# Maxima and scores of an attention step in another order on TensorE

## What is computed

```python
scores = jnp.einsum('bhqd,bhkd->bhqk', q, k) / np.sqrt(HD).astype(np.float32)
scores = jnp.where(attn_mask[:, None, None, :], scores, -jnp.inf)
attn = jax.nn.softmax(scores, axis=-1)
out = jnp.einsum('bhqk,bhkd->bhqd', attn, v)
out = out.transpose(0, 2, 1, 3).reshape(x.shape[0], x.shape[1], H)
x = residual + out @ wo + bo
...
ff = jax.nn.gelu(h @ ff_w1 + ff_b1, approximate=False) @ ff_w2 + ff_b2
return residual + ff
```

```python
scores = jnp.einsum('bqgrh,bkgh->bgrqk', q, k) * (1.0 / np.sqrt(HD))
a = jax.nn.softmax(scores, axis=-1)
out = jnp.einsum('bgrqk,bkgh->bqgrh', a, v).reshape(b, n, d)
...
x = x + g1 * _gqa_attn(h, wq, wk, wv, wo)
```

## Time and profile before

| | us |
|---|---|
| median of 3 runs | 4138.36 |
| lowest and highest | 4135.44 and 4140.47 |
| profiled execution, its own time | 4144.66 |
| its span from first to last instruction | 4142.9 |
| TensorE busy | 3823.0 |
| VectorE busy | 2498.1 |
| GpSimd busy | 1626.7 |
| ScalarE busy | 1605.7 |
| chain that ended last: TensorE, VectorE, issue, GpSimd | 76%, 13%, 4%, 3% |

### The profile page before, as it was taken

The page is one execution under the profiler, slowest core; times in us unless marked ns, Lnnn a source line. Parts: engine busy times, 40 slices in busy tenths (PEclk is TensorE's granted clock), DMA queues, the critical chain, the costliest instruction groups (busy, mean ns, idle before and its releaser), DMA issues.

```text
span 4142.9 us, 53495 instructions
## 1 busy us (share of the span) xinstructions
PE 3823.0 (92%) x20400; PEld 1511.9 (36%) x20400; DVE 2498.1 (60%) x3944; ACT 1605.7 (39%) x2807; POOL 1626.7 (39%) x907
## 2 busy tenths in 40 slices
PE   6898998998998989889899998999899998989999
PEld 4322443233533334333343333433244333433244
DVE  4687635767356764466654777367664776457752
ACT  1366312553125631155421663136521563126621
POOL 2377212673116742066510673026510573106620
PEclk9899999999999999999999999999999999999999
DMA  5233242221422223332222021311222112311112
GB/s 147 43 105 115 73 109 68 81 58 64 105 72 77 58 80 86 90 77 60 87 95 89 14 70 60 109 37 27 80 72 94 29 37 77 105 56 24 60 63 93
DMA packets 138973, 305.21 MB, mean 74 GB/s; under 512 B 19632, under 2 KB 59588, under 8 KB 137824
## 3 DMA queue, kind: packets, MB, share of 16 engines
q10 hardware_dynamic: 50944, 174.62, 13.0%
q1 hardware_dynamic: 87776, 127.17, 11.8%
HBM read 223.46 MB, written 36.66 MB: 63 GB/s over the span
## 4 chain that ended last, share of the span: by engine, by line
PE 76%; DVE 13%; issue 4%; POOL 3%; ACT 2%; DMA 1%; SPq 0%; ACTq 0%; DVEq 0%; POOLq 0%
PE ps L783 11%; PE ps L785 11%; PE ps L784 11%; PE ps L963 10%; PE ps L884 9%; PE ps L946 8%; PE ps L820 7%; PE ps L978 5%; DVE mcol L1443 3%; PE ps L837 2%; ACT probs L1125 2%; DVE turn L1365 1%; POOL sums L692 1%; DVE v_sb L1343 1%; PE ps L801 1%
## 5 line engine op out<-in xcount | busy, mean ns | idle before, releaser
L692 POOL TENSOR_TENSOR sums<-probs 128x1024 f32<-128x1024 f32 x480 | 1137.2, 2384 | 1393.0 <-ACT probs L1125 849.8
L1443 DVE TENSOR_REDUCE mcol<-ps 128x1 f32<-128x512 f32 x2048 | 1281.0, 683 | 368.5 <-PE ps L884 365.8
L1125 ACT ACTIVATE probs<-ps 128x512 f32<-128x512 f32 x2048 | 1100.5, 606 | 852.5 <-PE ps L946 625.9
L884 PE MATMUL ps<-ks,qs 97*128 97x512 f16 x2048 | 796.3, 395 | 126.2 <-DVE mcol L1443 76.0
L946 PE MATMUL ps<-qs,ks 98*128 98x512 f16 x2048 | 780.2, 392 | 78.0 <-ACT probs L1125 76.1
L1271 ACT ACTIVATE sums<-ps,cols 128x512 f32<-128x512 f32 x256 | 175.9, 687 | 1185.5 <-PE ps L785 1185.5
L963 PE MATMUL ps<-probs,v_sb 128*32 128x512 f32 x4096 | 560.1, 621 | 0.0
L884 PEld LDWEIGHTS ps<-ks,qs 97*128 97x128 f16 x2048 | 202.4, 99 | 708.2 <-DVE mcol L1443 436.1
L1534 DVE CAST probs<-sums 128x512 f16<-128x512 f32 x256 | 129.8, 507 | 485.7 <-ACT sums L1271 485.4
L783 PE MATMUL ps<-aT,ring 128*128 128x512 f16 x1024 | 395.2, 386 | 0.0
L784 PE MATMUL ps<-aT,ring 128*128 128x512 f16 x1024 | 394.0, 385 | 0.0
(11 more groups left out here) (107 smaller groups left out, 3286.5 us busy)
## 6 DMA issues: line engine op xcount, KB each, us to landing
ring<-halves ACTq DMA_DIRECT2D x208, 512.0 KB, 3.4
qs<-hl SPq DMA_DIRECT2D x192, 128.0 KB, 4.0
ring<-halves SPq DMA_DIRECT2D x48, 512.0 KB, 6.2
ring<-in_weights ACTq DMA_DIRECT2D x39, 512.0 KB, 4.3
halves<-ring ACTq DMA_DIRECT2D x37, 512.0 KB, 2.9
ks<-hl SPq DMA_DIRECT2D x120, 128.0 KB, 4.3
dcopy<-inverses SPq DMA_DIRECT2D x56, 256.0 KB
probs<-in_x SPq DMA_DIRECT2D x8, 1024.0 KB, 7.2
```

Source lines behind the costliest of these rows:

```text
L692: pool.tensor_tensor(sums[:, m % SUM_SLOTS, :, :], prob(u - 2), prob(u), ALU.add).then_inc(sum_set[0].sem, 1)
L884: pe.matmul(bank, qs[0:K_MAX, hh, h, P * qt:P * qt + P], ks[0:K_MAX, key_set(i, hh), key_head(i, hh, h), 512 * half:512 * half + 512], sta ...
L1125: act.activation(prob(u)[:, e, :], ps[:, w % SCORE_BANKS, :], ACT.Exp).then_inc(exp_done.sem, 1)
L1443: dve.tensor_reduce(mcol[:, blk % 2, 4 * j + qt, half:half + 1], src, AX.X, ALU.max).then_inc(n_free[0], 1)
```

## The change

In a step without a fill the order of TensorE was M0 S0 M1 S1 M2 S2 M3 S3, and a fifth maximum behind that. Now it is S0, then M0 and M1, then S1 and S2, then M2 and M3, then S3, and a fifth maximum behind that. In a step with a fill the order was M0 S0 M1 S1, fill, S2, fill, M2 S3 M3. Now it is S0 M0 M1 S1, fill, S2, fill, M2 M3 S3. Values, totals and row transposes stay where they were, and so does the program of every other engine. The order among the maxima and fills, which decides the banks, is the same.

```diff
                         maxima, fills = maxima_at(i, s), FILLS[i].get(s, [])
-                        some(maxima[0:1])
                         score(i, 4 * s)
-                        some(maxima[1:2])
+                        some(maxima[0:2])
                         score(i, 4 * s + 1)
                         for key in fills:
                             fill(key, 0, 6 if key[0] in "kqv" else 12)
-                        some(() if fills else maxima[2:3])
                         score(i, 4 * s + 2)
                         for key in fills:
                             if key[0] in "kqv":
                                 fill(key, 6, 12)
-                        some(maxima[2:3] if fills else maxima[3:4])
+                        some(maxima[2:4])
                         score(i, 4 * s + 3)
-                        some(maxima[3:] if fills else maxima[4:])
+                        some(maxima[4:])
```

## The result

| | before | after |
|---|---|---|
| median, us | 4138.72 (5 runs) | 4159.93 (5 runs) |
| lowest and highest of the new runs, us | | 4151.8 and 4164.18 |
| ratio, with its 95% interval | | 1.0049 (1.0033 to 1.0065) |
| profiled execution, its own time, us | 4144.66 | 4151.8 |

The account below looks back on a forecast made before the run. TensorE, busy 92% of the span and without holes inside attention steps, was taken as the bound. The terms 23.7 - 5.5 + 1 - 4 + 1 gave +16 us, so 4154.5 us, range 4143 to 4170.

Parts of the forecast that it names:

- M3 waits for M0's reduction: Ordinary attention steps on TensorE: M3, now five places behind M0, waits 0.07 us, making 0.08 us a step.
- How many steps pay: Ordinary attention steps: 285 pay 0.083 us each for M3's wait, +23.7 us (19 to 27).
- What comes back: In 44 ordinary steps S3's wait for S0's exponential swallows the maxima's delay, -5.5 us (between 3.7 and 7.3).
- S2 one place earlier: S2 waits for the previous step's S3 exponential: +1 us (0 to 2) in some 10 steps, elsewhere at most 0.04 us.
- pace-setting steps: Some 10 even steps of layer 0 where ScalarE sets the pace; each loses up to 0.18 us, +1 us (0 to 2).
- M0 behind S0: Where M0 waits at a step's start, S0 runs in that hole: -4 us (0 to -6).
- The other side: S0 of a new block waits for the maxima's row from memory, now a place earlier: +1 us (0 to 3).
- A sign that told nothing: TensorE's weight-load waits for the maxima's reductions were to rise in number, with one in nearly every ordinary step.
- No change: Rival: GpSimd's loop over the step pair forgives nearly all late even steps; 4138 to 4146 us, chance 0.13.
- Faster: Rival: earlier S0 shortens S3's 44 waits (-9.7 us) and M3's wait does not show; 4125 us, chance 0.06.
- A swinging clock through short waits: Rival: one in eight of 362 steps falls to TensorE's lower clock, 80 us, some 4235 us; chance 0.02.
- Long holds on VectorE: Rival: VectorE splits slide into GpSimd's additions at one to four places, +4 to +15 us, 4158 to 4170; chance 0.08.

Follow-up runs that it names:

- e4: Changed kernel with M2 and M3 ahead of S2 in steps without a fill, M0 and M3 four places apart: 4199.41 us, ratio 1.0143.
- e7: Changed kernel with each VectorE reduction reading 384 of 512 columns and 40 subtracted: 4116.7 us, ratio 0.9937.
- e2: Kernel before with only the first half of the change, S0 M0 M1 S1, then M2 S2 M3 S3: 4155.24 us, ratio 1.0040.
- e3: Kernel before with only the second half of the change, M0 S0 M1 S1, then S2 M2 M3 S3: 4154.27 us, ratio 1.0033.
- e1: Kernel before with the score first but maxima and scores still in turn, S0 M0 S1 M1 S2 M2 S3 M3: 4152.54 us, ratio 1.0026.
- e9: Changed kernel, unchanged, run again for a second trace: median 4163.55 us, ratio 1.0050; profiled execution 4164.1 us.
- e5: Kernel before, unchanged, run again for a second trace: 4144.0 us.
- e10: Changed kernel with the new order kept only in steps with a fill, the old order elsewhere: 4140.85 us, ratio 0.9996.
- e12: As e11, but with the fifth maximum left where it was: 4138.56 us, ratio 0.9991.
- e8: Kernel before with ScalarE's copy of the finished block one exponential later: 4134.8 us, ratio 0.9984.
- e11: e8 with S0 ahead of M0 in steps 0, 1, 2 and 8 and the fifth maximum of fill steps behind values and totals: 4143.66 us, ratio 1.0003.

## Why the prediction was right

**M3 waits for M0's reduction: right, and in its size.** Forecast were 1.17 us from M0 to M3 and a step of 2.93 us; both are in the rows to the hundredth. e4 doubles the cause (four places, +0.30 us against 0.30 worked out), e7 takes it away by a shorter reduction and the odd step is back at 3.69 us, e2 and e3 split the change by it. In layer 1, where chance is small, it accounts for the loss: 184 more steps start M3 on its release (192, before 8), 184 x 0.083 = 15.3 us, and S3's waits there fall by 3.4 us, from 5.8 to 2.4; that makes 11.9 us where 11.6 are measured.

**How many steps pay.** 285 were forecast. 329 now start M3 on its release, 31 did before, so 298 are new, 1.1 us more than the sum has.

**What comes back: right.** S3's waits fall, step 34 by 0.16 us. The block's +0.49 us is eight delays less two.

**S2 one place earlier: right for the change, for a reason that holds only there.** I wrote that it waits 0.04 us at most outside the pace-setting steps, and the rows have that. But I had not seen that this rests on M3's delay in the step before: that the term came out was luck. Without it (e3, e7) S2 waits 0.13 us in the even steps, a second loss (12.7 us in e3's median, some 10 in layer 1) that the first one hides. My expectation for e3 (0 to 3 us) and that for e1 (4 us faster) failed on it.

**M0 behind S0: not settled.** M0's waits for the rotated chunk fall from 10.2 to 8.5 us, and in the first steps from 15.6 to 9.9 us, but there S0 itself now waits 3.1 us. The rest of the span, outside the values of the sequences, is 1.8 us shorter in the first trace than in the first of before, and 1.9 us shorter in e9 than in e5; but the two traces of before differ by 2 us in it themselves. e10, which has this gain alone, and e12, which adds it to e8, show none that can be told from zero. The -4 us was at best a -2. The other side, S0 waiting for the row from memory, went from 4 waits and 1.8 us to 10 and 4.1: 2.3 us, where I took 1 (in e9 beside e5 1.7 us).

**The sum.** +16 was forecast, +20 (14 to 27) measured. Layer 1 gives 11.6 of it, layer 0 between -2.3 and +12 by the two traces, the rest -2. The missing 4 us are within the interval, and the two small terms just named with the 13 steps would account for some 4; the clock in layer 0 can do as much. It stays open which. The +1 us for S2 in the pace-setting steps was not told apart by any run. For the profiled execution I had 4161 us: the first took 4151.8, the second 4164.1, so one trace alone could have seemed to refute the sum.

**A sign that told nothing.** I wrote that the waits of the weight loads for the maxima's reductions would rise in number. They fell, from 685 to 505. At M3 they did rise, from 236 to 338 of the 362 steps, but those at M0 fell from 251 to 3, and 345 steps had such a wait before. What tells the two kernels apart is M3's start, 0.06 us after the reduction.

**The rivals.** No change: each even step has S3 on time, only those with the copy forgive. Faster: S0 of step 34 now stands a place earlier, but its exponential still follows the copy, at 2876.75, 1.23 us after the score; it is ScalarE that sets it, as I had put it. A swinging clock through short waits: with 184 more waits of 0.07 us in layer 1 its values are at the lower clock in step 60 of each sequence and nowhere else, as in both traces of before, so these waits do not touch the clock. The Trainium skill, page TensorE: Matmul & The Clock Gate, section A second HAM failure mode, would have short idles from cycling through banks make the clock swing; by waits of this length these traces do not bear it out. Long holds on VectorE: the splits of step 6 of sequences 0, 1 and 3 went from 1.2 to 3.2 us, so the crossing does happen, but it brought TensorE no long wait (steps 7 and 8 changed by 0.5 us at most), and all other splits changed by 0.4 us at most. e11 shows the mechanism at work where it does hurt.

## What to carry to other kernels

Where matmuls take turns in n banks that other engines empty, write down for each stream the loop time (start of the matmul, to the reader's start, its length, and the release) and the distance in slots to the n-th next of the same stream; an order is free only as long as every distance is longer than its loop. Two streams that pass through the same queue share one budget: pulling one forward takes a slot from the other, and a wait of one can hide the wait of the other, so halves of a reorder must be tried apart before their costs are believed. Waits much shorter than a matmul do not appear in a list of idle times (here some 300 of 0.07 us); compare start to start of one repeating step.

## What the runs showed of the hardware

A wait of 2.19 us on TensorE in the same place of the same program was followed once by matmuls at 2.4 GHz (granted clock 1.00, the values in 1.06 us) and once at 1.2 GHz (0.50, 1.94 us). Behind the 2.3 us of step 22 both traces of the kernel before had the lower level in three sequences and the full one in the fourth. This is a source of chance between executions: 14 us in layer 0 between two traces of the changed kernel, 2 us between two of the kernel before. Some 300 added waits of 0.07 us left the level alone.
